# A vision tower's routing: VectorE sums the tokens behind the norm's transposes and not at the head of the routing stage

## What is computed

```python
h = tok(x)                                  # patches @ W + b, class token, positions
h = h + attn0(layernorm(h))                 # one head, 192 wide, softmax
h = h + ffn0(layernorm(h))                  # routed: one of 3 experts for each image
h = h + attn1(layernorm(h))                 # 12 heads of 16
h = h + ffn1(layernorm(h))                  # patch tokens: fc1, gelu, fc2; 6 class tokens: routed atoms

# ffn0
scores = softmax(mean(x, axis=1) @ Wg.T)    # mean over the image's tokens
sel    = argmax(scores)
out    = scores[sel] * (gelu(x @ W1[sel] + b1[sel]) @ W2[sel] + b2[sel])
```

## Time and profile before

| what | value |
|---|---|
| median of 3 runs | 3438.12 us (3432.95 to 3445.44) |
| the profiled execution's own time | 3436.12 us |
| its span, first to last instruction | 3434.3 us |
| granted TensorE clock, mean | 0.932 of full speed |
| busy: PE, PEld, DVE, ACT, POOL | 2907.5, 2647.5, 2032.5, 1347.6, 356.6 us |

### The profile page before, as it was taken

One profiled execution on the slowest core, in us unless ns is written; L12 is line 12 of the kernel. 1 busy time (PEld: TensorE's weight loads), 2 busy tenths in 40 slices (PEclk: granted clock), 3 DMA queues, 4 the chain that ended last, 5 costly groups with the idle time before them and its releaser, 6 DMA issues.

```text
span 3434.3 us, 64029 instructions
## 1 busy us (share of the span) xinstructions
PE 2907.5 (85%) x23190; PEld 2647.5 (77%) x23190; DVE 2032.5 (59%) x5286; ACT 1347.6 (39%) x2840; POOL 356.6 (10%) x746
## 2 busy tenths in 40 slices
PE   4688888888888898888888988888898888888748
PEld 3588878877887787778878887788788778877646
DVE  4365566566656655666566656665655666566424
ACT  2144434444443344344434444443344444433311
POOL 0111111101111110111111101111111011110000
PEclk9699999999999999999999999999999999999868
DMA  5333443344243424433433344334433443333330
GB/s 148 81 66 90 91 89 71 85 98 96 64 92 83 93 65 96 96 74 82 98 82 77 81 96 96 72 84 93 87 68 88 98 96 67 89 84 83 59 87 4
DMA packets 127222, 287.54 MB, mean 84 GB/s; under 512 B 28790, under 2 KB 95367, under 8 KB 116172
## 3 DMA queue, kind: packets, MB, share of 16 engines
q1 hardware_dynamic: 127180, 286.97, 37.2%
HBM read 192.23 MB, written 15.00 MB: 60 GB/s over the span
## 4 chain that ended last, share of the span: by engine, by line
PE 46%; DVE 30%; DMA 9%; issue 6%; SPq 5%; ACT 3%; DVEq 0%; POOL 0%; POOLq 0%; ACTq 0%
PE banks L656 24%; PE banks L704 11%; DVE inv L1086 7%; DVE hx L981 5%; PE banks L809 4%; DMA shared<-low 4%; DMA shared<-nmaxT 4%; DVE nmax L1075 3%; DVE stats L967 2%; PE banks L827 2%; DVE sums L1084 2%; DVE xnT L1007 2%; SPq L525 2%; PE banks L680 1%; DVE low L1066 1%
## 5 line engine op out<-in xcount | busy, mean ns | idle before, releaser
L1075 DVE TENSOR_REDUCE nmax<-banks 99x4 f32<-99x788 f32 x384 | 360.7, 975 | 127.8 <-PE banks L809 122.5
L1251 ACT ACTIVATE probs_rest<-banks 99x396 f32<-99x396 f32 x512 | 246.0, 501 | 321.3 <-PE banks L827 320.0
L600 POOL TENSOR_TENSOR var_eps<-moments,eps 99x2 f32<-99x2 f32 x256 | 49.7, 194 | 2911.7 <-DVE moments L972 2911.7
L809 PE MATMUL banks<-shared,q_stack 128*99 128x198 f32 x1536 | 233.2, 290 | 91.2 <-DMA shared<-low 32.2
L827 PE MATMUL banks<-q_stack,shared 128*99 128x198 f32 x1536 | 285.6, 283 | 23.2 <-DMA shared<-nmaxT 19.1
L656 PE MATMUL banks<-tokT,fc_wT 128*128 128x198 f32 x1920 | 281.2, 302 | 5.1 <-DVE tokT L1007 5.0
L809 PEld LDWEIGHTS banks<-shared,q_stack 128*99 128x99 f32 x1536 | 188.1, 188 | 121.7 <-issue 63.9
L656 PE MATMUL banks<-tok_wT,xT 128*99 128x192 f32 x1536 | 273.3, 329 | 1.9 <-ACT xT L1207 1.9
L656 PEld LDWEIGHTS banks<-tokT,fc_wT 128*128 128x128 f32 x1920 | 260.8, 216 | 14.3 <-DVE tokT L1007 14.1
L1086 DVE RECIPROCAL inv<-sums 128x198 f32<-128x198 f32 x192 | 267.2, 1392 | 6.6
L704 PE MATMUL banks<-w_sb,hidT 128*99 128x192 f32 x1536 | 268.1, 326 | 0.0
(11 more groups left out here) (189 smaller groups left out, 5435.4 us busy)
## 6 DMA issues: line engine op xcount, KB each, us to landing
shared<-w_split SPq DMA_DIRECT2D x64, 1188.0 KB
xin<-in_x_dram SPq DMA_DIRECT2D x32, 1176.0 KB
w_sb<-in_L_ffn_W_dram SPq DMA_DIRECT2D x64, 576.0 KB, 6.1
w_last<-w_split SPq DMA_DIRECT2D x64, 384.0 KB
q_stack<-hi SPq DMA_DIRECT2D x128, 148.5 KB
q_stack<-low SPq DMA_DIRECT2D x128, 148.5 KB
shared<-hi SPq DMA_DIRECT2D x128, 148.5 KB
shared<-low SPq DMA_DIRECT2D x128, 148.5 KB
```

The source lines that it names most:

```text
L809: last = t_.matmul(b[n % 4][0:R, t * SP_:(t + 1) * SP_], q_stack[p][:, n, t * R:(t + 1) * R], k_stack[p][:, n, :], start=True, stop=True)
L1075: v.tensor_reduce(nmax1[p][:, :, 2 * j:2 * j + 2].rearrange("p t h -> p h t"), src, AX, ALU.max, negate=True).then_inc(nmax1_ready[p], 1)
L1251: s_.activation(ring(p, s).rearrange("p k s -> p (k s)"), b[s % 2][0:R, 0:T * SP_], ACT.Exp).then_inc(p1_ready[p], 1)
```

## The change

The token sum moves from the head of `route` to the end of `turn2` on VectorE, behind the remainders; the wait for `xnT_ready` in front of it goes. TensorE gets a wait for `xnT_ready` at the head of `v0` and of `v1`. The lists that set the order of stages are written in another way, and give the same order. Nothing else is changed; the line numbers of what follows fall by 10 to 15.

```diff
                 elif name == "v0":
+                    pe.wait_ge(xnT_ready[p], norm_count(1, it))
                     if not isinstance(it, int) or it:
                         pe.wait_ge(low_ready[p], 2 * it - 1)
                     values(p, it, b[1], attn_wv, tokT)
...
                 elif name == "v1":
+                    pe.wait_ge(xnT_ready[p], norm_count(3, it))
                     values(p, it, b[3], v_wT, xnT)
...
                             in1=b[TURN_BANK[n]][:, k * SP_:(k + 1) * SP_], op0=ALU.mult, op1=ALU.add)
                     last.then_inc(xnT_ready[p], 1)
+                    if n == 2:
+                        v.tensor_reduce(xsum[p][:], b[TURN_BANK[2]][:, 0:2 * SP_].rearrange("p (k s) -> p k s", k=2)
+                                        [:, :, 0:SEQ], AX, ALU.add).then_inc(xsum_ready[p], 1)
...
                 elif name == "route":
 
-                    dve.wait_ge(xnT_ready[p], norm_count(2, it))
-                    v.tensor_reduce(xsum[p][:], b[TURN_BANK[2]][:, 0:2 * SP_].rearrange("p (k s) -> p k s", k=2)
-                                    [:, :, 0:SEQ], AX, ALU.add).then_inc(xsum_ready[p], 1)
                     dve.wait_ge(logit_done[p], it + 1)
```

More of the change, by code:

```diff
@@ L51 @@
 REGROUPS = GRID // REGROUPED
[L58 to L77, removed]
+AHEAD = ["x", "tok0", "tok1", "stat1", "norm1", "turn1", "q0", "v0", "s0", "p0", "o0", "stat2", "norm2", "turn2", "route", "load"]
+FLOW = ("""hid0_0 hid0_1 hid0_2 out0_0 out0_1 stat3 x norm3 tok0 tok1 turn3 qk1_0 qk1_1 v1 stat1 norm1 turn1 q0 v0 max0
+        max1 max2 max3 max4 max5 maxT att0 s0 att1 att2 p0 att3 att4 o0 stat2 att5 att6 att7 norm2 att8 att9 att10
+        att11 att12 turn2 att13 route proj load stat4 norm4 turn4 hid1_0 hid1_1 hid1_2 out1_0 out1_1""")
+STAGES = [(n[:3], int(n[3:])) if n[:3] in ("att", "max") and n != "maxT" else n for n in FLOW.split()]
 B_FIRST = 30
```

## The result

The changed kernel takes 3449.7 us (median of 10 runs, 3445.2 to 3453.3) against 3442.0 for the kernel before in the same comparison. The ratio is 1.0023, with a 95% interval from 1.0013 to 1.0034: by the 0.3% that the prediction takes as its bound no change, and by the interval slightly slower, by 0.2%. Measured once more in a later comparison it was 1.0026 (1.0013 to 1.0039). 3398 us was forecast, a gain of 1.2%, with a range that ends at 3434. The profiled execution took 3446.3 us, 10.2 more than the one before, and its mean granted clock is 0.909 instead of 0.932.

The account below looks back on a forecast made before the run. TensorE, busy 85%, shares the path with VectorE and waits 134.6 us for the token sum. 3436.1 - 53 won + 13 given back to the clock = 3396, stated as 3398 us; range 3362 to 3434.

Parts of the forecast that it names:

- (1): TensorE at the routing: its wait for the token sum goes, logits follow `v1` directly, projection waits 0.9 us at most.
- (2): VectorE: the sum's 0.53 us only move, the 0.82 us wait before `logit` goes; transposes start 1.9 us earlier.
- (3): Attention maxima: 1.8 us arrive in 24 halves B (side 0 routes), 0.5 in 7, 0.2 per half A; 53 us won.
- (4): Stacking transfers on SyncE: the earlier expert weights' load does not push them back; costed at nothing, bounds 0 to 33 us.
- (5): TensorE's added waits in `v0` and `v1`: met long before, taken as nothing; other end 20 us.
- (6): Clock behind half A's maxima: moved idle time gives back a quarter of the gain, 13 us; ends nothing and 65 us.
- The rival drawn from it: Behind the maxima: moved idle time ends in a slow stretch in every half A; 3450 us, chance 0.03.
- VectorE is the bound: VectorE: the sum ahead of the head products makes each of 64 places 0.53 us later; 3472 us, chance 0.04.
- The gain is eaten: Half A's idle time ahead of the maxima ends slow in half the pairs, 47 us against 53; 3432 us, chance 0.12.
- All of it, and the clock too: Nothing given back, 3385 us; 3354 if the ten slow stretches behind half A's maxima go too; chance 0.25.

Follow-up runs that it names:

- e1: Kernel before with only TensorE's two added waits (in `v0` and `v1`), the sum left where it was: 3447.7 us, ratio 1.0002.
- e6: Changed kernel with filling matmuls, whose results are unused, ahead of the transposes of norm 1 and `q0`, not ahead of the maxima: 3420.6 us, ratio 0.9946.
- e8: Kernel before with only side 1's sum moved (halves A), side 0's left in place: 3453.4 us, ratio 1.0056.
- e9: Changed kernel with filling matmuls only ahead of the maxima, 10 in half A and 4 in half B: 3346.7 us, ratio 0.9736.
- e2: Changed kernel with TensorE held ahead of the routing matmuls until VectorE reaches routing, so the old stall returns: 3438.4 us, ratio 0.9980.
- e4: Kernel before with only the stall ahead of the routing matmuls filled, 16 matmuls in half B and 14 in half A: 3417.6 us, ratio 0.9933.
- e11: Kernel before with filling matmuls only ahead of the maxima, 7 in half A and 4 in half B: 3433.5 us, ratio 0.9955.

## Why the prediction was wrong

*(1) and (2), the steps on TensorE and VectorE, were right.* The stall went; the projection waits 0.46 us for the head products (0.9 at most was said); the norm starts 1.17 us behind `logit` (1.16); the transposes win 2.2 us (1.9). The sum takes 561 ns in its new place, not 534. (The 0.30 us that the prediction reads for the earlier trace rows is the wait of the weight load there; the matmuls' own row has none.)

*(3), how much reaches the maxima, was too high.* 1.5 us in half B and 0.2 in half A were counted, 53 us in all; 1.13 and 0.20 came, 41 us in 31 pairs. Where half B runs at full clock up to its maxima, in 18 of 29, it gets the 12.6 us, as the earlier trace rows said. Where it doesn't, `v0` or `q0` and `v0` are slow, in the other 11: I had checked the clock behind the old stall and behind the maxima, and not between.

*(4) and (5) were right.* In half A the stacking holds the maxima at 12.67 us, although the load now goes out earlier; the added waits cost nothing (e1).

*(6) is the step that failed.* "I take a quarter of the gain as given back": 13 us were counted, and 1.62 us a pair came behind the maxima, 50 us. With 12 us less won and 37 us more given back, 40 us faster became 9 slower. Four things in the step were off. The clock was priced for half A alone; half B has it too, 0.92 us a pair. It may be that its waits for the norm and ahead of `q0` stand close together now: filling these two took the slow stretches out of half B (e6). But e8 has them there with half B's order untouched, so this is not shown to be the only way. The count before was of long slow stretches only, ten; with the short ones it is 16 of 29 halves A, and 29 of 29 after. And the share itself, a quarter, came from no row. The price of 3.1 us went the other way, and was too high: with a slow stretch in all 29, half A takes 34.70 us behind its maxima against 32.78 with the clock kept (e9), 1.9 us each. The kernel before already paid 1.2 us of this.

The idle time of half A lies otherwise than before: 1.69 us ahead of the transposes and 1.39 ahead of `q0` (the rows of e9, which keeps these two), or 2.88 us ahead of the maxima, and every half A has a slow stretch behind its maxima. The rule that stood beside the step is in the Trainium skill, "TensorE: Matmul & The Clock Gate", section "Part 1: The HAM clock gate (the "warmup" mystery)": the throttled state is the default and activity lifts it. The trace of e9 agrees: 0.59 while the filling ran in half A, 1.00 in the 16 us behind. The rival drawn from it gave 3450 us; I had given it 0.03. That it meets the measured 3449.7 is in part luck: it had the stretch in every half A right, but it counted 53 us won and 65 given back, all of the 65 in half A, where 41 and 50 came, more than half of the 50 in half B.

The rivals: "VectorE is the bound" is wrong (e2). "The gain is eaten" is what happened, in both halves and by more than the gain. "All of it, and the clock too" (3385, and 3354 at its end) did not come by itself; it is about where the changed kernel goes once filling keeps the clock: 3347 and 3348 us.

What stays open: why one order of the slow stretches settles in and not another, and what exactly lowers the clock. In e8 nearly every pair is alike; in the kernel before and in the changed one long, short and no stretches take turns. The spread of runs in e4, e6 and e11 (37, 33 and 35 us, against 5 us in the two kernels with everything filled and 8 in the changed one) suggests that several patterns can hold; no run here chose between them. The table has one execution of each kernel, so its tenths bear less weight for these three.

## What to carry to other kernels

When a change takes a stall away in front of one piece of work but another limit, here a DMA, holds the next, the idle time moves and does not go; read the granted clock behind the place it moves to before counting the gain. In this kernel a slow stretch cost nothing where there was slack (e9, at `q0` and `v0`) and 1.0 to 1.9 us on average where work was dense (behind the maxima of half B and half A). If idle time has to be somewhere, a few matmuls right ahead of the dense part can be the cheapest instructions of the kernel: here the filling alone made it 0.45% faster (e11), the reordering alone 0.2% slower, and both together 2.6% faster (e9).

## What the runs showed that was not expected

448 matmuls that compute nothing (14 in a pair, e9) made the changed kernel 2.9% faster, 3446.9 to 3346.7 us, although they ran at half clock themselves in 21 of 29 halves A. And a change in one half of the loop moved the slow stretches of the other: with only half A's sum moved, the slow time behind the maxima of half B went from 0.8 to 4.3 us, and the whole loss stood there.
